# Rounding the gated rows with one two-step VectorE instruction instead of ScalarE and VectorE in turn, with the five order lists written anew

## The reference

```
def act_quant(x):
    scale = 127.0 / clip(max(abs(x), axis=-1), 1e-05)
    return clip(round(x * scale), -128, 127) / scale

h = bit_linear(x, w1)            # 256 -> 1024, both sides rounded
h = depthwise_conv1d(h)          # three taps over the tokens
h = silu(h)
return bit_linear(h, w2)         # 1024 -> 256: h is rounded again, here
```

## Time and profile before

| | |
|---|---|
| median of 3 runs | 3401.01 us (3395.61 to 3408.89) |
| the profiled execution, its own time | 3401.43 us |
| its span, first to last instruction | 3399.6 us |
| TensorE matmul busy | 2940.5 us, 86% |
| TensorE weight load busy | 2079.4 us, 61% |
| VectorE busy | 2539.8 us, 75% |
| ScalarE busy | 2179.9 us, 64% |
| GpSimd busy | 752.2 us, 22% |
| mean granted TensorE clock | 0.960 of full speed |

### The profile page before, as it was taken

The page is one execution under the profiler, slowest core; times in us unless marked ns, Lnnn a source line. Parts: engine busy times, 40 slices in busy tenths (PEclk is TensorE's granted clock), DMA queues, the critical chain, the costliest instruction groups (busy, mean ns, idle before and its releaser), DMA issues.

```text
span 3399.6 us, 59753 instructions
## 1 busy us (share of the span) xinstructions
PE 2940.5 (86%) x23277; PEld 2079.4 (61%) x23404; DVE 2539.8 (75%) x5468; ACT 2179.9 (64%) x4270; POOL 752.2 (22%) x1360
## 2 busy tenths in 40 slices
PE   2589996999879998899988998889988999889984
PEld 2446664667646666567665676656665676656763
DVE  5565579765897669975798758976699757987576
ACT  2237864477756776567765677657775677656773
POOL 0341012410143102331123201421023311232000
PEclk9789997999999999999999999999999999999996
DMA  4100000000000000000000000000000000000000
GB/s 140 32 1 1 1 12 17 17 1 1 15 22 9 1 4 23 12 9 1 15 12 20 1 4 12 23 9 2 4 23 12 9 1 15 12 20 1 1 1 13
DMA packets 46092, 45.14 MB, mean 13 GB/s; under 512 B 11136, under 2 KB 43776, under 8 KB 45680
## 3 DMA queue, kind: packets, MB, share of 16 engines
q1 hardware_dynamic: 40928, 35.72, 3.6%
q10 hardware_dynamic: 4880, 5.58, 0.5%
HBM read 32.90 MB, written 8.39 MB: 12 GB/s over the span
## 4 chain that ended last, share of the span: by engine, by line
PE 59%; DVE 24%; ACT 10%; issue 4%; POOL 3%; SPq 1%; DMA 1%; DVEq 0%; POOLq 0%; ACTq 0%
PE banks L1166 9%; PE banks L1197 9%; PE banks L1243 6%; PE banks L1305 4%; PE banks L1206 4%; DVE chain_m L685 4%; PE banks L1182 3%; PE banks L1239 3%; PE banks L1269 3%; DVE chain_arena L877 2%; PE banks L1387 2%; DVE chain_arena L761 2%; PE banks L1284 2%; ACT chain_arena L1000 2%; PE banks L1329 2%
## 5 line engine op out<-in xcount | busy, mean ns | idle before, releaser
L1197 PE MATMUL banks<-chain_arena 64*128 64x256 f32 x3072 | 439.6, 408 | 39.2 <-DVE chain_m L685 28.2
L685 DVE TENSOR_REDUCE chain_m<-banks 128x4 f32<-128x512 f32 x512 | 329.2, 682 | 113.4 <-PE banks L1197 112.5
L1197 PEld LDWEIGHTS banks<-chain_arena 64*128 64x128 f32 x3072 | 274.4, 190 | 168.1 <-issue 86.1
L1496 POOL TENSOR_SCALAR chain_ng<-chain_sv 128x2 f32<-128x2 f32 x192 | 52.6, 274 | 1448.8 <-DVE chain_sv L666 1448.7
L1021 ACT ACTIVATE chain_arena<-chain_arena,chain_m 128x128 f32<-128x128 f32 x1024 | 323.9, 392 | 27.4 <-DVE chain_m L685 24.7
L955 ACT ACTIVATE chain_xn<-chain_xa,chain_nm,chain_rs 128x256 f32<-128x256 f32 x384 | 209.3, 596 | 162.2 <-POOL chain_nm L1500 161.4
L1243 PE MATMUL banks<-chain_arena 64*128 64x256 f32 x2048 | 294.9, 407 | 0.0
L681 DVE TENSOR_TENSOR chain_arena<-banks,pos_bias 128x512 f32<-128x512 f32 x256 | 174.9, 683 | 105.7 <-PE banks L1197 105.5
L1243 PEld LDWEIGHTS banks<-chain_arena 64*128 64x128 f32 x2048 | 178.9, 188 | 122.5 <-issue 110.6
L1206 PE MATMUL banks<-chain_arena,chain_va 128*32 128x128 f32 x5120 | 195.3, 278 | 35.8 <-ACT chain_arena L1000 23.4
L1000 ACT ACTIVATE chain_arena<-banks,chain_mask_k 128x1024 f32<-128x1024 f32 x128 | 142.4, 1114 | 103.4 <-PE banks L1243 102.6
(11 more groups left out here) (309 smaller groups left out, 7021.1 us busy)
## 6 DMA issues: line engine op xcount, KB each, us to landing
chain_xn<-in_ctx SPq DMA_DIRECT2D x32, 256.0 KB, 2.7
chain_xa<-in_x SPq DMA_DIRECT2D x32, 256.0 KB, 3.1
out<-chain_xa SPq DMA_DIRECT2D x32, 256.0 KB, 2.1
chain_arena<-in_mask SPq DMA_DIRECT2D x32, 128.0 KB, 3.6
rel<-in_rel SPq DMA_DIRECT2D x1, 2048.0 KB, 8.7
f_w1t<-in_w1t ACTq DMA_DIRECT2D x1, 1024.0 KB, 11.8
f_w2t<-in_w2t ACTq DMA_DIRECT2D x1, 1024.0 KB, 14.8
wqkv0T<-in_wqkv0T ACTq DMA_DIRECT2D x1, 768.0 KB, 10.9
```

The source lines that it names most:

```text
L685: e.tensor_reduce(m, s.rearrange("p (j o) t -> p j o t", o=2), AX.X, ALU.max, negate=True).then_inc(*done(f"{tag}_mx{u}"))
L1197: mm[i] = e.matmul(c.ps[:, i, 2 * T * j:2 * T * j + 2 * T], t["qh"][p, j, x, b, :], flat(t["kx"][p, j, b]), start=not masked, stop=not mas ...
```

## The change

It takes L1143 off ScalarE, and L895 becomes one VectorE instruction with two arithmetic steps. It waits for the multiplication of its own engine and no longer for ScalarE. The two event names `g_ro0` and `g_ro1` go out of the table of ScalarE, whose turn has 79 steps instead of 81.

```
@@ mlp_vector
     for b in range(B):
-        e.wait_ge(*act(f"g_ro{b}"))
-        e.tensor_scalar(t["hq"][:, :, b, :], cv[:, :, b, :], -ROUND, None, ALU.add).then_inc(*done(f"g_r2{b}"))
+        e.wait_ge(*dve(f"g_mu{b}"))
+        e.tensor_scalar(t["hq"][:, :, b, :], cv[:, :, b, :], ROUND, -ROUND, ALU.add, ALU.add).then_inc(*done(f"g_r2{b}"))
         yield
@@ scalar_turn
     gate(HT // 2 - 1)
     yield
-    for b in range(B):
-        v = t["cv"][:, :, b, :]
-        e.wait_ge(*dve(f"g_mu{b}"))
-        e.activation(v, v, ACT.Identity, bias=k["rounder"][:, 0:1]).then_inc(*done(f"g_ro{b}"))
-        yield
@@ ORDER, all five strings new from their first digits; two lines of them
     "vector": (
-        "3012333333000300031110222131133221332023313030021300320112201012021331121023232103321332000000112200"
+        "0123000000111011102221323223001300330110010110211301012132210022330023300211030211232113323211332222"
```

More of the change, by code:

```diff
@@ L98 @@
     "sync": (
[L99 removed]
+        "0011223301021323001213230012132300121323001213230012132300121323"),
     "pool": (
[L101 to L103 removed]
@@ new lines @@
+    "scalar": (
+        "0123001012023013110202213301321323002031110022201031031030110201021012020231031021302131321010301202"
+        "3021310200102301310023002103102113001030213200011013021201231131203102232312110130102212233231321220"
+        "2330233130112302202332030323031332132010231002100201010313003133021121221211223213131302132231230002"
+        "3202002321033232133213111033131330002122222030203023030213011303003011031210122001101003030021312012"
+        "0020102120013001230312030300210213200230010213103131121021031213011300122331221312110203130113130312"
+        "2021230332032322012133232231320121030330232320020123310032301031213201123122331301131001120121012021"
+        "1220123033233032322312223121313213201023301321333320300100002022210212010320332033320103110311131002"
+        "0200120101001303132010200202020103012321032030030210213210321123111312310230213011301022313122131211"
+        "0203130113130312202123033203232201213323223132012103033023232002012331003230103121320112312233130113"
+        "1001120121012021122012303323303232231222312131321320102330132133332030010000202221021201032033203332"
+        "0103110311131002020012010100130313201020020202010301232103203003021021321032112311131231023021301130"
+        "1022313122131211020313011313031220212303320323220121332322313201210303302323200201233100323010312132"
+        "0112312233130113100112012101202112201230332330323223122231213132132010233013213333203001000020222102"
+        "1201032033203332010311031113100202001201010013031320102002020201030123210320300302102132103211231113"
+        "1231023021301130102231312213121102031301131303122021230332032322012133232231320121030330232320020123"
+        "3100323010312132011231223313011310011201210120211220123033233032322312223121313213201023301321333320"
+        "3001000020222102120103203320333201031103111310020200120101001303132010200202020103012321032030030210"
+        "2132103211231113123102302130113010223131221312110203130113130312202123033203232201213323223132012103"
+        "0330232320020123310032301031213201123122331301131001120121012021122012303323303232231222312131321320"
+        "1023301321333320300100002022210212010320332033320103110311131002020012010100130313201020020202010301"
+        "2321032030030210213210321123111312310230213011301022313122131211020313011313031220212303320323220121"
+        "3323223132012103033023232002012331003230103121320112312233130113100112012101202112201230332330323223"
+        "1222312131321320102330132133332030010000202221021201032033203332010311031113100202001201010013031320"
+        "1020020202010301232103203003021021321032112311131231023021301130102231312213121102031301131303122021"
+        "2303320323220121332322313201210303302323200201233100323010312132011231223313131111212121231213213233"
+        "2332322232233232233232332333"),
```

151 lines of the change are left out of this document (64 added, 87 removed).

## The result

The changed kernel takes 3430.71 us (median of 4 runs, 3426.51 to 3432.3), against 3402.19 for the kernel before on the same chip: ratio 1.0078, 95% interval 1.0058 to 1.0098. It is slower, by more than 0.5%, where 3366 us and 1.0% faster were forecast; 3430.71 also lies above the upper end of the range, 3416.

What follows compares the result with a forecast made beforehand. TensorE was taken to bound the repeating part nine tenths of the time. Start 506, second turn 396, six periods 2361.6, tail 97 and 3.3 made a span of 3363.9; with 1.8 around it 3366 us, range 3330 to 3416.

Steps and rivals of the forecast that it cites:

- What bounds the kernel now: Repeating part: TensorE busy 91% of a 396.1 us period; its 36.2 idle us spread thin over waits on ScalarE and VectorE.
- Part 1, the ScalarE instruction: Removing L1143 frees ScalarE 14.5 us per period, worth 0.9 us per period through TensorE's 17.5 us of waits on ScalarE.
- Part 2, the second step at no cost: VectorE's L895: a second arithmetic step costs 0 over 64 instructions; at the slower rate it would cost 33.5 us on VectorE.
- Part 3: Path through the rounding: the first rounding gains 0.1 to 0.2 us; direct gain 0.2 us at the end.
- Part 4, start, second end, tail: New lists outside the full periods: start unchanged at 506 us, first to second end 396, tail 97 where 129.5 stood.
- Two side by side fill each other's gaps: In the tail, the blocks g of chains 2 and 3 run together in 53 us, VectorE busy for 47.
- Six full periods: Repeating part under the new lists: six periods of 393.6 us, 2361.6 in all; ends for the range 388 and 402.
- P: Length of one full period of the repeating part: 396.1 us in four periods before, 393.6 forecast.
- The rival that VectorE becomes the bound: Chains 2 and 3 running block g at once crowd VectorE: period 402.5 us, time 3420; chance 0.15.

Runs made afterwards that it cites:

- e1: The changed instructions with the order lists of the kernel before, less the two ScalarE digits of each turn: 3400.33 us, ratio 0.9986 to the kernel before.
- e2: The instructions of the kernel before with the change's new lists, the two ScalarE digits put back: 3449.9 us, ratio 1.0141 to the kernel before.
- e4: The changed kernel with its new lists, three VectorE instructions of block g cut to a fraction of their columns: 3396.78 us in one run.
- e12: The changed kernel with chain 3 moved to end its turn some 47 us behind chain 2, then all lists re-sorted: 3392.19 us, ratio 0.9971 to the kernel before.
- the control: The changed kernel with the close pair of chains kept, all lists re-sorted by the same number of small moves: 3391.43 us, ratio 0.9965 to the kernel before.
- e11: The changed instructions with the old lists re-sorted by small moves, carried on further: 3348.56 us, ratio 0.9846 to the kernel before.
- e14: The changed kernel with chain 3 moved to end its turn some 32 us behind chain 2, then all lists re-sorted: 3415.63 us, ratio 1.0033 to the kernel before.
- e5: The changed kernel with all five engines' new lists re-sorted by small moves, the close pair kept: 3370.89 us, ratio 0.9914 to the kernel before.
- e8: The changed kernel with VectorE's list alone re-sorted by small moves, the other four as in the change: 3503.17 us in one run.

## Why the prediction was wrong

- **"What bounds the kernel now"**: right in what it says. TensorE is the bound nine tenths of the time and the rest is thin; the 10 us that a period grew are again such waits.
- **Part 1, the ScalarE instruction**: right in kind under the old lists. ScalarE 2117.4 us where 2107 was forecast. e1's trace shows a turn of 396.2, so nothing of the 0.9 us per period; by the medians the edit gave some 5 us in all, which 0.9 x 8 would be, where 64 x 1148 ns were taken off ScalarE. (The execution of e1 that was traced took 3407.15 us, 7 above its median.) Under the new lists the same edit gave some 20 us, more than Part 1 has.
- **Part 2, the second step at no cost**: right. L895's median is 686 ns, its mean over 64 is 701, as this row of the kernel after shows, and VectorE's total fell by 5.6 us:

```profile
L895 DVE TENSOR_SCALAR chain_arena<-chain_arena 128x1024 bf16<-128x1024 f32 x64 | 43.1, 701 | 0.0
```

  Its maximum is 861 ns, so the lengthened ones cost 64 x 15 ns = 1 us, not 4. In the traces 8 of the 64 took over 720 ns before, 6 now and 13 in e1, and every one of them ran beside a GpSimd instruction. (That fits with the rule of the Trainium skill, "SBUF — State Buffer", "Who interferes with whom", by which a two-port tensor_scalar and GpSimd lock each other out: 28 of the 64 met GpSimd before, 13 now. Under the old lists, e1, the mean is 764.)
- **Part 3**: the direct gain at the end is below what these runs can show.
- **Part 4, start, second end, tail**: near, 494.3 for 506, 388.4 for 396, 92.5 for 97, each better than forecast. The start was to stay "unchanged" by its count of digits and fell by 12 us; e2, with the old instructions, has 494.7, so the new lists made that. (The lower bound of the tail, 47 and 36 x 1.1, adds up to 87, not 88; nothing hangs on it.) "Two side by side fill each other's gaps" holds: 51.4 us with VectorE busy for 45.11, 88%.
- **Part 4, "Six full periods"**: this step failed. It took P = 393.6 "half-way to 391.1", from a stretch of the old lists that happened to be 5 us better, and said that one 5 worse "is as easy". P was 406.0 to 412.6, 12 to 19 above and 15.2 in the mean, times six: the 91 us. With the instructions the same, the lists alone make some 30 us of the time (e1 to the change). Two things were wrong in it. The distance an order can be off was taken from the one pair of rows at hand; the twelve versions here that leave no work out gave 388 to 421, with TensorE busy for 357 to 370 us of them. And the sign was taken from a purpose ("the lists, made for a ScalarE with 5% less to do"): whatever use they make of the 14.5 freed us (the edit is worth more under them, e2), they lose more elsewhere, and TensorE's waits on ScalarE rose from 17.5 to 20.8.
- **The rival that VectorE becomes the bound**: right in place, and what the prediction said to look for came, turns above 399, VectorE 47.64 and TensorE 33.20. Its time (3420) is near by luck: P rose by 12.7 us, twice what it took (402.5), and the 24.5 us that start, second turn and tail came in under the forecast hid much of that. Its mechanism fell with e4, and e12 found no gain in taking away its cause, the close pair. A rival can fit every row it asked for and not be the cause.

What stays open: which trait of the new lists makes the loss. Re-sorted, they came to turns of 396 to 400 at best and the old ones to 388 to 393; whether the new arrangement can be brought there by other moves was not tried beyond these.

## What to carry to other kernels

Where several chains share engines in a fixed order, an edit and a new order are two changes: measure each alone, since here the edit was worth -5 us and the order +48, and they don't add up: together they made +29. Don't price a new order by its count of digits or by the load of the engines it relieves; only the second turn and the tail came within 8 us of such counts. A deep dip of the bounding engine can show where lateness is collected and not where it is made: re-sorting only the dip gave nothing, flattening it gave nothing over the control, re-sorting everything else gave 42 us. And one re-sorting is one draw: two with the same arrangement differed by 20 us.

## What the runs showed of the hardware

The granted clock changes with the order. In the dip of the change it is 0.92 and 0.91 of full speed, in e4's 0.86, while the rows of the same period with TensorE above 45 of 50 us show 1.00. Inside the dip it falls to half behind the long waits:

```profile
2606.60:2618.00 11.40, 4.97 (x30) 2.36 (x30) 11.37 (x24) 3.83 (x7) 0.87 (x2) 1.00 0.01 2
2618.00:2631.70 13.70, 9.67 (x68) 5.72 (x70) 13.39 (x21) 5.30 (x6) 0.85 (x3) 0.50 0.00 0
```

So a TensorE that waits also gets longer matmuls: the 2048 of L1238 take a mean of 418 ns in the change and 402 in e11:

```profile
L1238 PE MATMUL banks<-chain_arena 64*128 64x256 f32 x2048 | 304.6, 418 | 0.0
```

```profile
L1238 PE MATMUL banks<-chain_arena 64*128 64x256 f32 x2048 | 290.4, 402 | 0.0
```

That is 14 us of busy time for the same work. In the change 120 of the 2048 fall where the clock is half and take a mean of 671 ns; the other 1928 take 402, as all 2048 do in e11. How idle TensorE must be doesn't show: a stretch of e14 with 32.93 busy of 50 us has a clock of 0.97. Not expected either was how much a shift of single steps by about one place is worth, up to 60 us (e5) in 3430, nor that a change to one engine's string alone can cost 72 us (e8).
